# A vision tower on one core: the second attention and the graph stage in one block, a node table without the turned tokens, and the scores ahead of the sort

## The reference, cut to what matters

```python
def step(carry, v_prev):                       # L1 attention, 64 steps per image
    x_state, rho = carry
    x_t = 0.97 * x_state + relu(v_prev @ Dx.T)
    x_t = x_t / max(sum(abs(x_t)), 1e-12)
    y_t = relu(ln(rho @ x_t) @ Dy.T) * relu(x_t)
    v_star = ln(y_t @ E.T)
    rho_t = 0.97 * rho + outer(ln(v_prev), x_t)
    return (x_t, rho_t), v_star
h = layernorm(h + L1_attn(h))
# L1 feed-forward: a graph softmax over 262144 edges decides between 4 experts
hg = (x @ W_gat).reshape(M, 4, 4)
a_src, a_dst = (hg * att_src).sum(-1), (hg * att_dst).sum(-1)
e = leaky_relu(a_src[src] + a_dst[dst], 0.2)
alpha = softmax of e over the edges of each dst
agg = segment_sum(hg[src] * alpha, dst) + b_gat
w = softmax of the top 2 of the layer-normed scores, 0 for the others
out = sum over experts of w[e] * (gelu(x @ W1[e] + b1[e]) @ W2[e] + b2[e])
h = layernorm(h + out)
```

## Time and profile before

| | |
|---|---|
| median of 3 runs | 957.71 us (957.58 to 965.55) |
| profiled execution | 966.87 us, its span 965.0 us |
| DVE busy | 601.5 us (62%) |
| PE busy | 447.3 us (46%) |
| ACT, POOL busy | 231.8 us, 209.3 us |
| granted TensorE clock, mean | 0.683 of full speed |
| DMA | 13.18 MB, mean 14 GB/s |

### The profile page before, as it was taken

The page is one execution under the profiler, slowest core; times in us unless marked ns, Lnnn a source line. Parts: engine busy times, 40 slices in busy tenths (PEclk is TensorE's granted clock), DMA queues, the critical chain, the costliest instruction groups (busy, mean ns, idle before and its releaser), DMA issues. The chain is left out here.

```text
span 965.0 us, 10711 instructions
## 1 busy us (share of the span) xinstructions
PE 447.3 (46%) x3501; PEld 346.0 (36%) x3501; DVE 601.5 (62%) x2282; ACT 231.8 (24%) x488; POOL 209.3 (22%) x214
## 2 busy tenths in 40 slices
PE   5994576326946699587996413000000219600000
PEld 5774576115932255366882402000000217500000
DVE  4999999377768999565788437522223002371487
ACT  2688773108122222230011121000000022200121
POOL 0000000000000000100000057777777600007404
PEclk9997877676577899786679556555555559555555
DMA  8100000000000000000000110111111300011002
GB/s 177 31 2 1 2 1 2 8 0 2 3 1 1 0 2 1 7 16 1 0 1 1 15 32 10 10 10 10 10 10 10 42 1 1 0 66 10 7 0 43
DMA packets 30779, 13.18 MB, mean 14 GB/s; under 512 B 25321, under 2 KB 30057, under 8 KB 30449
## 3 DMA queue, kind: packets, MB, share of 16 engines
q1 hardware_dynamic: 21664, 9.04, 3.8%
q0 software_dynamic: 6144, 2.37, 3.6%
q10 hardware_dynamic: 2904, 0.98, 0.7%
HBM read 8.48 MB, written 3.90 MB: 13 GB/s over the span
## 5 line engine op out<-in xcount | busy, mean ns | idle before, releaser
L1940 POOL DMA_INDIRECT gathered<-node_table,list_src_i x160 | 157.5, 985 | 50.5 <-issue 50.5
L1982 PE MATMUL bank<-e_w,e_hidden 128*128 128x64 f32 x256 | 38.1, 322 | 175.7 <-issue 174.6
L1982 PEld LDWEIGHTS bank<-e_w,e_hidden 128*128 128x128 f32 x256 | 37.2, 236 | 179.4 <-issue 177.2
L406 ACT ACTIVATE dst_one_hot<-dst_lo,sign_edges 128x256 bf16<-128x256 bf16 x224 | 90.8, 511 | 16.6 <-PE bank L463 16.6
L463 PE MATMUL bank<-dst_one_hot 128*128 128x128 bf16 x1024 | 71.0, 241 | 39.3 <-DVE dst_one_hot L533 39.3
L2148 DVE SCALAR_TENSOR_TENSOR bank<-list_node_one_hot,node_rows_own,bank 128x192 f32<-128x192 bf16 x124 | 43.3, 418 | 69.9 <-remote 64.5
L463 PEld LDWEIGHTS bank<-dst_one_hot 128*128 128x128 bf16 x1024 | 69.6, 110 | 40.7 <-DVE dst_one_hot L533 40.3
L533 DVE TENSOR_SCALAR dst_one_hot<-dst_hi 128x256 bf16<-128x256 bf16 x512 | 76.0, 359 | 0.3 <-ACT edge_keys_then_tokens L390 0.3
L2300 DVE TENSOR_TENSOR expert_out<-bank,e_b 128x512 f32<-128x512 f32 x16 | 11.0, 691 | 76.2 <-PE bank L1982 39.9
L1951 POOL DMA_INDIRECT node_rows<-segment_table,segment_end_i x32 | 30.5, 953 | 107.9 <-DMA segment_table<-segment_rows 98.5
L1969 PE MATMUL bank<-h_features,e_w 64*128 64x512 f32 x64 | 26.3, 909 | 47.9 <-ACT e_hidden L2002 23.9
(11 more groups left out here) (430 smaller groups left out, 1064.6 us busy)
## 6 DMA issues: line engine op xcount, KB each, us to landing
gathered<-node_table,list_src_i POOLq DMA_INDIRECT x160
segment_table<-segment_rows SPq DMA_DIRECT2D x3, 768.0 KB
dst_one_hot<-in_L_ffn_edge_index SPq DMA_DIRECT2D x2, 1024.0 KB, 7.3
out_dram<-edge_keys_then_tokens SPq DMA_DIRECT2D x4, 256.0 KB, 2.6
images_then_col_weights<-in_x SPq DMA_DIRECT2D x2, 441.0 KB
images_then_col_weights<-in_x ACTq DMA_DIRECT2D x2, 441.0 KB
e_w<-in_L_ffn_W SPq DMA_DIRECT2D x6, 128.0 KB
node_rows<-segment_table,segment_end_i POOLq DMA_INDIRECT x32
```

The source lines that it names most:

```text
L406: ins = act.activation(hot[q % 2][:, :, 64 + HOTS + k, :], x, ACT.Sign, bias=edge[:, k:k + 1])
L1940: pool.indirect_dma_start(Gt[:, j, :], None, A["table"], bass.IndirectOffsetOnAxis(ap=G.src_i[:, j:j + 1], axis=0)).then_inc(gat[g // per_ ...
L1982: ins = pe.matmul(G.bank[6 + n % 2][:, (u * EXP1 + e) * D:(u * EXP1 + e + 1) * D], HH[:, u, e, h * P:(h + 1) * P], W2[:, e, :], start=True ...
```

## The change

Three edits. **Scores first:** in the first attention DVE takes the row maxima and folds weights ahead of `sort_batch`, and divides the attention output ahead of the one-hots; the last four one-hot rounds go behind the sums of squares. **Second attention:** its weights are loaded by SP at the end of the block before (`Attention1Weights`). The rates are computed on 96 partitions (three copies of the 32 chunks, from a wider `pick`), split into three bf16 parts that add up to the f32 value, and spread by bf16 matmuls with a one-hot of 96 rows; own and decay rates go to banks of their own, so that DVE multiplies and scans 512 columns at a time. The node table is no longer made from the turned tokens of `lnh`: since the layer norm is linear up to its scale, it is made as (tokens times `Wg`, computed after the sums of the states, plus v times `Wg` times `lnw`'s scale) times `lnh`'s scale, and is written before `lnh.apply` and the turn. **One block:** `attention1`, `graph_fill` and `graph_and_experts` return parts that run in one block, without barriers between. The expert weights are loaded at its start, the constants set up while DVE would wait for the sums; large buffers of the graph stage are views of buffers of the attention.

```diff
@@ first attention, DVE @@
                 w.constants(dve)
-                sort_batch(f0)
                 for g in range(NG):
                     dve.wait_ge(s_mm, g + 1)
...
                 w.fold(dve, G.ident)
                 dve.sem_inc(folded, 1)
+                sort_batch(f0)
...
-                o = Steps(dve, own, early * PER)
-                bins(o)
-                for j in range(RB):
-                    one_hots(o, j)
-
                 dve.wait_ge(s_exp, NC)
...
                     dve.tensor_tensor(R[:, c, :], R[:, c, :], HV[:, c, 0:D], ALU.add).then_inc(ln0.x_ready, 1)
+                o = Steps(dve, own, early * PER)
+                bins(o)
+                for j in range(RB - 4):
+                    one_hots(o, j)
                 ln0.add_squares(dve)
                 ln0.sum_ready_for_act(dve)
+                for j in range(RB - 4, RB):
+                    one_hots(o, j)
                 parts_of_keys(o)
@@ first attention, SP, last @@
+                G.a1.load(A, sp, a1_in)
@@ second attention, SP @@
+        load_list(G, A, sp, 0, scattered, list_in)
+        G.load_experts1(sp)
+        sp.wait_ge(tab_s, 1)
@@ second attention, PE @@
-                pe.wait_ge(par_in, 96)
-                pe.wait_ge(ones_s, 1)
...
         sums(NG - 1).then_inc(sum_mm, 1)
+        pe.wait_ge(wg_s, 1)
+        table_of_tokens(0, NC // 2).then_inc(tok_mm, 1)
         pe.wait_ge(rate_s, 1)
         def spread(k):
             for i in range(CPT):
                 c = k * CPT + i
-                ins = pe.matmul(G.bank[2 * (k % 2) + i // 2][:, (i % 2) * 2 * P:(i % 2 + 1) * 2 * P],
-                                G.ident[0:NC, c:c + 1].to_broadcast([NC, P]),
-                                rates[:, :, :].rearrange("c r t -> c (r t)"), start=True, stop=True)
+                for r in range(2):
+                    ins = pe.matmul(G.bank[2 * (k % 2) + r][:, i * P:(i + 1) * P],
+                                    of_chunk[:, c:c + 1].to_broadcast([3 * NC, P]), parts[:, r, :], start=True,
+                                    stop=True)
...
         v_to_tokens(3)
+        pe.wait_ge(pair_s, 1)
+        for k in range(NG):
+            ins = table_of_v(k)
+        ins.then_inc(row_mm, 1)
         th.tensor(pe, G)
-                pe.wait_ge(wg_s, 1)
-                th.wait(pe)
-                for i in range(NC // 2):
-                    for u in range(2):
...
+        def table_of_v(k):
+            for i in range(CPT):
+                c = k % 2 * GC + 2 * i
+                ins = pe.matmul(G.bank[k // 2][:, c * ROW:(c + 2) * ROW], VT[:, k, i * P:(i + 1) * P],
+                                Wg_pair[:, :, :].rearrange("p u f -> p (u f)"), start=True, stop=True)
@@ second attention, ACT: v_std first, then Relu; after them @@
+        act.wait_ge(tok_mm, 1)
+        for odd in range(2):
+            act.copy(tok_rows[:, odd::2, :], G.bank[6 + odd][:, 0:NC // 2 * ROW].rearrange(
+                "p (c f) -> p c f", f=ROW)).then_inc(tok_s, 1)
@@ second attention, DVE @@
+        G.fill_vector(dve)
+        G.set_up_constants(dve)
         dve.wait_ge(sum_mm, 1)
...
+        o.then(dve.tensor_copy(parts[:, :, :], rates[:, :, :]))
+        middle, low = slice(NC, 2 * NC), slice(2 * NC, 3 * NC)
+        o.then(dve.tensor_tensor(rates[:, :, :], rates[:, :, :], parts[:, :, :], ALU.subtract))
+        o.mark(dve.tensor_copy(parts[middle, :, :], rates[middle, :, :]))
+        o.then(dve.tensor_copy(parts[low, :, :], rates[low, :, :]))
+        o.then(dve.tensor_tensor(rates[low, :, :], rates[low, :, :], parts[low, :, :], ALU.subtract))
+        o.then(dve.tensor_copy(parts[low, :, :], rates[low, :, :]))
...
+            for g in range(NH2):
+                o.mark(dve.tensor_tensor(x[g], x[g], own_rate[:, :], ALU.mult))
+            o.wait()
+            for g in range(NH2):
+                o.mark(dve.tensor_tensor_scan(x[g], decay_rate[:, :], x[g], 0.0, ALU.mult, ALU.add))
...
+        dve.wait_ge(row_mm, 1)
+        for b in range(2):
+            c = slice(b * NC // 2, (b + 1) * NC // 2)
+            o.mark(dve.tensor_tensor(G.tab[:, c, :], G.bank[b][:, 0:NC // 2 * ROW].rearrange(
+                "p (c f) -> p c f", f=ROW), lnw.inv[:, c].unsqueeze(2).to_broadcast([P, NC // 2, ROW]), ALU.mult))
+        o.wait()
+        dve.wait_ge(tok_s, 2)
+        o.then(dve.tensor_tensor(G.tab[:, :, :], G.tab[:, :, :], tok_rows[:, :, :], ALU.add))
+        lnh.add_squares(dve)
+        lnh.sum_ready_for_act(dve)
+        lnh.invert(dve)
+        dve.tensor_tensor(G.tab[:, :, :], G.tab[:, :, :], lnh.inv[:, :].unsqueeze(2).to_broadcast([P, NC, ROW]),
+                          ALU.mult).then_inc(tab_s, 1)
+        lnh.apply(dve)
         th.vector(dve, G)
@@ graph stage, DVE @@
         dve.sem_inc(list_ready, 1)
+        dve.wait_ge(G.tab_s, 1)
+        G.turned.wait(dve)
         set_up(dve, o)
@@ program @@
-        attention1(nc, G, A)
-        graph_fill(nc, G, A)
-        graph_and_experts(nc, G, A)
+        attention, fill, graph = attention1(st, G, A), graph_fill(st, G, A), graph_and_experts(st, G, A)
+        with nc.Block() as block:
+            @block.vector
+            def _(dve):
+                attention.dve(dve)
+                graph.dve(dve)
...
```

More of the change, by code:

```diff
@@ L170, in stage, with sync, gpsimd, tensor @@
     return st
+class Part:
+    def sync(self, f):
+        self.sp = f
+    def gpsimd(self, f):
+        self.pool = f
+    def tensor(self, f):
+        self.pe = f
+    def scalar(self, f):
+        self.act = f
+    def vector(self, f):
+        self.dve = f
 def new_semaphore(nc, G, name):
@@ L224, in scale, with invert, apply @@
     def scale(self, dve):
+        self.invert(dve)
+        self.apply(dve)
+    def invert(self, dve):
         dve.wait_ge(self.std_ready, 1)
         self.steps.then(dve.reciprocal(self.inv[:, :], self.std[:, :]))
+    def apply(self, dve):
         for g in range(LG):
@@ L1375, in _, with __init__, load @@
                 e.then(dve.tensor_copy(G.mean_sq[:, :], mean_sq[:, :]))
+class Attention1Weights:
+    def __init__(self, st):
+        self.DxT, self.DyT = st.sb("dx_t", [P, NSTATE]), st.sb("dy_t", [P, NSTATE])
+        self.Ew, self.decay = st.sb("e_w", [P, NH2, D]), st.sb("decay", [P, P])
+        self.Wg, self.att = st.sb("gat_w", [P, ROW]), st.sb("gat_att", [P, 2, HEADS * EXP1])
+    def load(self, A, sp, loaded):
+        for u in range(2):
+            r = rows_of(u)
+            sp.dma_start(self.DxT[r, :], A["L1_attn_DxT"]).then_inc(loaded, 16)
+            sp.dma_start(self.DyT[r, :], A["L1_attn_DyT"]).then_inc(loaded, 16)
+            sp.dma_start(self.Wg[r, 0:16], A["L1_ffn_W_gat"]).then_inc(loaded, 16)
+        sp.dma_start(self.Ew[:, :, :], A["L1_attn_ET"].rearrange("(g p) d -> p g d", g=NH2)).then_inc(loaded, 16)
+        sp.dma_start(self.decay[:, :], A["c_decay"]).then_inc(loaded, 16)
+        for i, n in enumerate((A["L1_ffn_att_src"], A["L1_ffn_att_dst"])):
+            sp.dma_start(self.att[:, i, :], n.rearrange("(o h) e -> o (h e)", o=1).to_broadcast([P, 16])
+                         ).then_inc(loaded, 16)
+        sp.wait_ge(loaded, 160)
 def load_list(G, A, eng, k, to, list_in):
```

1637 lines of the change are left out of this document (824 added, 813 removed).

## The result

The changed kernel takes 925.38 us in the median of 4 runs (923.78 to 925.91), the kernel before beside it 961.63 (957.58 to 967.42): ratio 0.9616, interval 0.9552 to 0.9680. The forecast was 912.5 in a range of 889 to 932. The profiled execution, 923.78 with a span of 921.8, is 43.2 us shorter in its span than the one before; 45.2 had been forecast for it.

A forecast was written before the change was run, and what follows sets the result against it. No engine was busy much over half the span; POOL's 160 gathers were taken to set the end. Terms of −40.2 and −5 on 965.0 gave 919.8, profiled 921.7, less the 9.2 offset 912.5 us in the median; range 889 to 932.

The forecast's parts named there:

- First gather: POOL's first gather of the node table: at 523.4 instead of 563.6, 40.2 us earlier by the stages ahead.
- scores first: First attention: row maxima ahead of the sort bring the turned features' copy from 272.1 to 264.3, −7.8 us.
- Weights and rates: Start of the second attention: weights loaded early, token table beside the rates' chain; loop starts 5.25 us earlier.
- Loop: Second attention's loop over states: PE's f32 spreads hold it; bf16 spreads and 512-column steps save 10.6 us.
- Table: Node table made from values instead of turned tokens: 6.35 us from the norm's sums instead of 16.7, −10.35 us.
- One block: Between node table and first gather: merging blocks leaves 6.2 us of 12.25, −6.0 us.
- that case: First attention: PE's count rounds wholly at 1.2 GHz take 21 us, end at 265 and cost 1 us.
- the 5 us: After the first gather: DVE's head start before the slow phase, kept as −5 us, bounds 0 and −21.
- Rival (a): After the first gather: head start kept in full, another −8 to −16 us, 897 to 905; chance 0.12.
- (c): After the first gather: DVE's steps slow from that gather on, all 32 nodes at 5.6 us, 936; chance 0.07.
- Rival (d): Chunks 1 and 2: the slow state doesn't end, 72 DVE steps cost 1.0 us more each, 987; chance 0.06.
- rival (b): Ahead of the table: two of loop at 47, sort edit worth 0, one block at 10; 924 to 928; chance 0.13.

The follow-up runs named there:

- half_nodes: The changed kernel with only 16 of the 32 nodes of the list worked out; median 917.48 us, ratio 0.9610 to the kernel before.
- gathers_128: The changed kernel without the 32 gathers of chunk 2, whose rows stay at zero; median 886.75 us, ratio 0.9281 to the kernel before.

## Why the prediction was right, point by point

- **First gather:** forecast 40.2 us earlier (the terms add to 40.0), measured 43.3. By its terms: scores first 7.8, measured 6.7 (the wait of 6.6 came as 6.51; PE's count rounds were no wait any more; DVE's pause behind the sort, 3.13 us before, came as 4.39). Weights and rates 5.25, measured 13.1 − 6.7 = 6.4. Loop 10.6, measured 13.8. Table 10.35: from 507.71 to 514.01 are 6.3 us, forecast 6.35, and before 16.7. One block 6.0: from the table to the first gather 6.3, forecast 6.2; of these, 5.1 us pass from the issue of the table's write (514.04) to that of the load which waits for it (519.14).
- **Two slips in its sums, without weight.** The new work ahead of the rates adds to 1.6 + 3.7 + 3.2 = 8.5 us, not 8. And 17.5 us at a granted clock of 0.78 would be 27 us at 1.2 GHz if all of it scaled with the clock, not 21, so that case would have cost about 7 us and not 1; it didn't come, the rounds' clock was 0.85.
- **The loop's mechanism failed in part.** The step said that PE's f32 spreads held it, and that the scores cost what they did. The runs put 2.0 us on the spread alone, 4.1 on DVE's wide instructions alone, 8.4 on both. The rest, 5.4 us, goes with a granted clock of 0.60 that rose to 0.79, and with the width and the banks of the spreads; its cause stays open. DVE's prices were right (a multiply 0.64 us, a scan 1.17 in a pair); what was too high was the pace, 4.40 us for the 4.6 of a group, and the tail. The Trainium skill, TensorE: Matmul & The Clock Gate, section "HAM oscillation — how this bites in real kernels", lets PE fall back to 1.2 GHz after idle gaps, and by that the scores would have become dearer. They became cheaper, 327 ns for 387, with 11.5 us of gaps in 37. The trace agrees in part: the clock did fall to half once in this loop, for about 6 us. But it was half for longer in the loop before, where PE had no gaps, so gaps alone don't tell the clock here. The page's case, a wait for a transfer longer than the matmuls around it, isn't in this loop.
- **After the first gather the forecast kept 5 us, and nothing was kept** (+0.75). The argument that the end is tied to the gathers was right, and half_nodes and gathers_128 show it; the 5 us contradicted it. Their premise, that the pauses begin at the same time after the gathers (+51), failed as well: they began at +45, behind the same 56 sums. Rival (a), the head start kept in full, fell by the same runs, and (c), slow from the first gather on, by the 56 unhindered sums. Rival (d), that the slow part doesn't end, fell: the rest takes 174.5 us, before 175.2. The fourth output, at +227.0, is a little outside the 221 to 226 named as its sign.
- **That the span is only 2.0 us off is in part luck.** The loop and the weights gave 4.4 us more than forecast, the scores 1.1 less, and the 5 us after the first gather didn't come: errors of opposite signs.
- **The median was mis-sized by 12.9 us.** 2.1 are from the profiled time. The other 10.8 are the offset of 9.2 that was taken off between profiled execution and median, and 1.6 more, as here the profiled execution is that much below the median of its kernel. The offset was no fixed property of a kernel. The tail of 87 to 97 us is of the right size for it and was long in the execution before; in the changed kernel it was long as well, and its four runs lie within 2.1 us. That the runs differ by their tails is argued, not shown. The first three runs (two at 957.6, one at 965.6) already showed that there was more than one value. So the median fell outside the likeliest band, 903 to 922, and into the 924 to 928 of rival (b), though none of (b)'s conditions came true: the loop took 37.0 us, the sort's edit gave 6.7, one block took 6.3.

## What to carry to other kernels

Find what ends last in each stage and treat the stages ahead of a long queue of transfers as one sum: here every microsecond before the first gather came off the end, and of some 90 us less work of DVE's behind it no more than 6, until gathers were left out or the work behind them was put in another order. Where two engines hold a loop nearly level, cost both: undoing either edit alone shows only its small part. Don't carry an offset between one profiled execution and a median over to another kernel before you have found which stretch makes it.

## What the runs showed of the hardware

While POOL's indirect gathers are under way, what waits for another instruction can come late on all engines, although the instructions take no longer. DVE comes to one signalled instruction in about 1.4 us: a node of 4 sums in 5.6 us, of which the sums take 1.40. PE does 16 matmuls in 7.09 us, by 718.6, and the two outputs that they make are seen at 731.12 and 747.27, 16 us apart; ACT's next GELU starts 28.7 us after the last of them. It ends 1.41 to 1.42 us x the number of gathers after the first (160, 128 and 32 of them: 227, 182 and 45 us). It begins about 20 us into DVE's sums, behind 56 of them in every kernel that has the pauses, be that 45, 51 or 55 us after the first of 160 gathers; with 32 gathers beside the experts it began about 23 us after the first. In one group of four kernels it didn't occur, and the time of the kernel before was 80 us lower. Whether it comes from how completions are reported or from the transfers themselves was not tried, nor what sets its beginning.
